# Target rows of a graph layer by one fp32 product a tile instead of three bf16 products

## The chip, the cores and the metric

The kernel runs on one core of a Trainium2 chip. The metric is the time of one execution in device microseconds.

## The reference, cut to what matters

Two graph layers stand behind each other on 3125 nodes of 256 features with 53125 edges, sorted by target node (`dst`). The change lies in the first layer, where each edge needs the projected row of its source and that of its target:

```python
ZU = jnp.einsum('nd,kdr->knr', Z, U)          # K=4 heads of R=16, so 64 numbers a node
zs = ZU[:, src, :]
zd = ZU[:, dst, :]
logits = (zs * zd).sum(-1) / scale
seg_max = jax.vmap(lambda l: jax.ops.segment_max(l, dst, num_segments=N))(logits)
exp_l = jnp.exp(logits - seg_max[:, dst])
seg_sum = jax.vmap(lambda e: jax.ops.segment_sum(e, dst, num_segments=N))(exp_l)
alpha = exp_l / (seg_sum[:, dst] + 1e-16)
agg = jax.vmap(lambda w_: jax.ops.segment_sum(w_, dst, num_segments=N))(alpha[..., None] * zs)
```

A dense gradient step and a layer norm follow on the nodes. The second layer sums rows of neighbours and runs a GRU cell on them.

## The kernel before

The nodes are cut into 25 windows (t = 0 to 24) of W = 125 targets. Since the edges are sorted by target, the edges of a window are one piece of the list, of at most SPAN = 2304, worked on as C = 18 tiles of 128 edges. The program is unrolled over the windows, `overlapped(attend)` on DVE and ACT and a plain loop on TensorE, and each engine has its order written out. Buffers alternate between two halves, h = t % 2.

In the first layer, for each window:

- GpSimd (`gather`, L638) fetches the source rows `zs` with one indirect transfer a tile, 18 a window, as soon as the indices `sidx` of the window are there. DVE writes those of window t + 2 (`sources`, L963) behind V of window t.
- SyncE (`prefetch`, L490 and L492) loads the target numbers of a window, the same row into 125 partitions (`dst_bc[h]`, 1125 KB), and pieces of them (`halo_i`). It waits for the one-hot of window t before it loads window t + 2 and then stores the finished rows of window t (`store_h2`, L509) before it turns to the next.
- DVE makes from `dst_bc[h]` the transposed one-hot `ohT` in bf16 (`target_one_hots`, L924), 125 nodes by 2304 edges. There is one such buffer. It also splits the 64-number rows of the window's own nodes, fp32, into three bf16 parts whose sum they are (`split_rows`, L929 to L937, five operations, each waiting for the one before it). Both are done one window ahead.
- TensorE multiplies the one-hot of each tile with the three parts and adds them up in fp32 (`target_rows`, L1600): 54 products for a window, into banks 0, 1 and 2. This picks each edge's target row.
- DVE `attend`: in three chunks of 8, 8 and 2 tiles it multiplies source and target rows (L954) and sums by head into `L` (L957). Between the chunks stands the end of the preceding window (`renew`, `shift`, L1057 to L1071). TensorE turns L (L1609), DVE runs two scans for the segment maxima (L995, L997, L1001), makes the next window's one-hot (L924), a remainder for the second layer (L915) and, once TensorE has turned the maxima back (L1612), the difference (L1008). ACT takes the exponential (L1334). DVE scales the source rows with it into V (L1013), writes indices (L963), compares neighbours for the next window (L941), and makes the node one-hots `oh` of the next window (L892).
- TensorE behind L1612: the dense part (L1637), the next window's target rows (L1600), and the aggregation `oh` by V (L1623, 18 products), which waits for V and for `oh` of its own window.
- DVE waits for that sum (L1038), divides, and starts the first chunk of the next window (L954).

In the last window TensorE has no target rows to make, and DVE makes two long one-hots of the second layer (L907) ahead of the first chunk. In the first window DVE splits weights for the second layer ahead of it. TensorE's queue in the first layer is thus: turn a row (L1630), L1609, L1612, L1637, L1600, L1623, L1641, L1643.

## Time and profile before

| | |
|---|---|
| time, median of 3 runs | 1218.3 us (1218.26 to 1241.45) |
| time of the profiled execution | 1217.22 us |
| its span, first to last instruction | 1215.6 us |
| busy: TensorE products, loads | 853.1 us (70%), 640.5 us (53%) |
| busy: DVE, ACT, GpSimd | 682.5 us (56%), 293.9 us (24%), 563.5 us (46%) |
| first layer's windows, about | 137 to 799 us |
| first-layer gathers on GpSimd (L638) | 450, 534.5 us busy |
| target rows (L1600) | 1350 products, 85.3 us busy |
| one-hot for them (L924) | 25, 35.3 us busy |

A product's weight load is a record of its own (PEld) and runs beside products. An fp32 product of this kernel leaves two records of each kind where a bf16 product leaves one: L1623 has 18 products a window and 36 records. In a row of the timeline, x is the number of records that were merged, and the bracket is the idle time of the engine in front of them with what ended it; "issue" is no wait that the profile shows. The two levels of TensorE's clock are 1.2 and 2.4 GHz; 0.5 and 1.0 stand for them in a stretch.

### The profile page before, as it was taken

Reading aid. Unit: us, or ns where it says so; the run is one execution under the profiler, and the core shown is the slowest. Engines: PE = TensorE matmul, PEld = TensorE weight load, DVE = VectorE, ACT = ScalarE, POOL = GpSimd, SP = SyncE. Lnnn points to the kernel's source line nnn. Section 1 sums busy time; section 2 is a strip of 40 time slices with the busy share of each in tenths; the row PEclk is TensorE's granted clock in tenths of the full one; section 3 lists DMA queues with packets and bytes.
Section 4 is the critical chain, followed back from the end, with each engine's and each line's share of the span. In section 5 each row is a group of like instructions: output and inputs, shape, how many; then the busy total and the mean of one; then the engine's idle time right before and its main releaser. Section 6 shows DMA issues by size and latency. Waiting matters only on the chain.

```text
span 1215.6 us, 14336 instructions
## 1 busy us (share of the span) xinstructions
PE 853.1 (70%) x5247; PEld 640.5 (53%) x5247; DVE 682.5 (56%) x1264; ACT 293.9 (24%) x621; POOL 563.5 (46%) x495
## 2 busy tenths in 40 slices
PE   0451656667655666665556666569999999999997
PEld 0341444456544455544445555446666666676764
DVE  4452566664565664455556555545566666555562
ACT  5230111111111111111111111224333333344331
POOL 3537277787778787777787877300000000000000
PEclk9985655555555555555555555569999999999999
DMA  4226233334333333332333331000000000000000
GB/s 126 79 48 128 81 72 69 73 79 95 73 70 71 73 81 82 78 68 68 71 71 74 80 84 35 12 13 18 17 15 16 13 18 17 18 17 18 18 14 14
DMA packets 42545, 65.97 MB, mean 54 GB/s; under 512 B 14247, under 2 KB 31696, under 8 KB 39350
## 3 DMA queue, kind: packets, MB, share of 16 engines
q1 hardware_dynamic: 24843, 48.23, 12.0%
q0 software_dynamic: 16576, 16.76, 11.0%
q8 instruction: 42, 0.69, 0.3%
q14 instruction: 28, 0.23, 0.1%
q10 hardware_dynamic: 1056, 0.07, 0.1%
HBM read 57.69 MB, written 7.20 MB: 53 GB/s over the span
## 4 chain that ended last, share of the span: by engine, by line
POOL 42%; PE 35%; issue 13%; DVE 4%; SPq 3%; DMA 2%; ACT 1%; POOLq 0%; DVEq 0%; ACTq 0%
POOL shared L638 40%; PE bank L1671 11%; PE bank L1670 5%; PE bank L1714 4%; PE bank L1721 4%; PE bank L1655 3%; PE bank L1722 2%; PE bank L1715 2%; DVE layer L1076 1%; DVE layer L1078 1%; POOL oh L712 1%; PE bank L1519 1%; PE bank L1682 1%; DMA layer<-in_edges,row_at 1%; DMA rels<-in_L_gnn_relvectors 1%
## 5 line engine op out<-in xcount | busy, mean ns | idle before, releaser
L638 POOL DMA_INDIRECT shared<-zu_table,sidx x450 | 534.5, 1188 | 162.9 <-issue 136.5
L1623 PE MATMUL bank<-layer,oh 128*125 128x84 f32 x900 | 192.1, 412 | 0.0
L1623 PEld LDWEIGHTS bank<-layer,oh 128*125 128x125 f32 x900 | 187.9, 326 | 0.0
L1600 PE MATMUL bank<-zu,shared 125*128 125x64 bf16 x1350 | 85.3, 238 | 78.8 <-issue 43.5
L1600 PEld LDWEIGHTS bank<-zu,shared 125*128 125x128 bf16 x1350 | 74.7, 127 | 102.4 <-issue 102.3
L1038 DVE TENSOR_SCALAR den<-bank 125x4 f32<-125x4 f32 x25 | 4.1, 162 | 189.9 <-issue 129.7
L1609 PE MATMUL bank<-ident,L 128*72 128x128 f32 x75 | 21.0, 417 | 125.6 <-DVE L L957 68.8
L1076 DVE COPY layer<-bank 125x256 f32<-125x256 f32 x25 | 10.6, 424 | 141.0 <-PE bank L1671 141.0
L907 DVE TENSOR_TENSOR shared<-iota_b,key_col 128x3125 bf16<-128x3125 bf16 x25 | 85.2, 3409 | 0.0
L907 DVE TENSOR_TENSOR oh<-iota_b,low_col 128x3125 bf16<-128x3125 bf16 x25 | 85.2, 3409 | 0.0
L1609 PEld LDWEIGHTS bank<-ident,L 128*72 128x72 f32 x75 | 9.4, 159 | 135.6 <-DVE L L957 73.8
L1362 ACT ACTIVATE cnt_rows<-meansT 51x125 bf16<-51x125 f32 x25 | 7.6, 305 | 281.7 <-issue 175.7
L1655 PEld LDWEIGHTS bank<-shared,oh 128*125 128x125 bf16 x625 | 61.7, 142 | 23.9 <-issue 10.0
L1655 PE MATMUL bank<-shared,oh 128*125 128x125 bf16 x625 | 66.5, 225 | 10.0 <-issue 9.0
L1671 PE MATMUL bank<-wide,zus 125*125 125x512 bf16 x208 | 73.3, 389 | 0.0
L1392 ACT ACTIVATE zus<-bank 125x500 bf16<-125x500 f32 (+1 forms) x91 | 60.3, 688 | 41.8 <-PE bank L1655 41.8
L1392 ACT ACTIVATE shared<-bank 125x500 bf16<-125x500 f32 (+1 forms) x84 | 55.8, 685 | 50.3 <-PE bank L1655 50.3
L1671 PE MATMUL bank<-wide,shared 125*125 125x512 bf16 x192 | 65.6, 379 | 0.0
L892 DVE SCALAR_TENSOR_TENSOR oh<-iota_w,win_first,dst_col 128x2250 f32<-128x2250 f32 x25 | 63.8, 2552 | 0.0
L954 DVE TENSOR_TENSOR layer<-shared,bank 128x512 f32<-128x512 f32 (+1 forms) x75 | 41.2, 549 | 37.1 <-DMA shared<-zu_table,sidx 33.3
L1670 PE MATMUL bank<-wide,zus 125*125 125x256 bf16 x195 | 54.3, 278 | 0.0
L1714 PE MATMUL bank<-whhT,layer 128*125 128x512 f32 x100 | 51.1, 593 | 0.0
(227 smaller groups left out, 1513.4 us busy)
## 6 DMA issues: line engine op xcount, KB each, us to landing
shared<-in_edges SPq DMA_DIRECT2D x25, 1125.0 KB
shared<-zu_table,sidx POOLq DMA_INDIRECT x450
xs<-in_x SPq DMA_DIRECT2D x5, 625.0 KB
h_table<-h2s SPq DMA_DIRECT2D x25, 125.0 KB
h2s<-h_table SPq DMA_DIRECT2D x25, 125.0 KB
out_dram<-layer SPq DMA_DIRECT2D x25, 125.0 KB
halo_i<-in_edges SPq DMA_DIRECT2D x25, 108.6 KB
zu_table<-zus SPq DMA_DIRECT2D x5, 156.2 KB
```

The costliest lines, as they stand in the source:

```text
L638: nc.gpsimd.indirect_dma_start(out=to(h, j), out_offset=None, in_=table, in_offset=bass.IndirectOffsetOnAxis(ap=sidx[:, h, j:j + 1], axis= ...
L892: nc.vector.scalar_tensor_tensor(o, in0, win_first[:, bass.ds(t, 1)], col, ALU.add, ALU.is_equal).then_inc(oh_made, 1)
L907: nc.vector.tensor_tensor(to.rearrange("p (g w) -> p g w", g=BW), io, col[:, t * BW:(t + 1) * BW].unsqueeze(2).broadcast_to([128, BW, W]), ...
L954: nc.vector.tensor_tensor(prod[:, a * KR:b * KR], zs[h][:, a * KR:b * KR], ps(c, 128, 0, (b - a) * KR), ALU.mult).then_inc(prod_made, 1)
L1392: nc.scalar.activation(many[t % 2].rearrange("p (a g d) -> p g a d", a=NW, g=BW)[:, a:b, :, :], ps((7, 1)[g % 2], W, 0, (b - a) * W).rearr ...
L1600: last = mm(ps(c, 128, (j - a) * KR, (j - a + 1) * KR), ohT[:, j * 128:(j + 1) * 128], zu3[:, m, :], start=m == 0, stop=m == 2)
L1623: last = mm(ps(5, W, 0, SUMS), oh[:, h, j * W:(j + 1) * W], V[:, j, :], start=j == 0, stop=j == C - 1)
L1655: last = mm(ps((7, 1)[g % 2], W, (k - a) * W, (k - a + 1) * W), lows[t % 2][:, k * W:(k + 1) * W], keys[t % 2][:, k * W:(k + 1) * W], star ...
L1670: mm(ps(0, W, 0, D), own, v[:, 2, :], start=False, stop=False)
L1671: last = mm(ps(0, W, 0, 2 * D), own, v[:, 0:2, :].rearrange("p m d -> p (m d)"), start=a == 0, stop=a == NW - 1)
L1714: mm(ps(rzb, W, 0, 2 * D), h2T[:, c * W:(c + 1) * W], whhT[:, c, 0:2 * D], start=False, stop=False)
L1721: mm(ps(rzb, W, 0, 2 * D), redT[:, c * W:(c + 1) * W], wihT[:, c, 0:2 * D], start=False, stop=c == CH - 1)
```

## The change

The one-hot is written as fp32 over the target numbers that it is made from: `ohT[h]` is `dst_bc[h]`, read as fp32. So there are two of them now. The five operations of `split_rows`, their buffers `zu3` and `rest` and their semaphore are gone. `target_rows` multiplies each tile's fp32 one-hot with the window's fp32 rows `zus`, one product a tile, 18 for a window. Since the next load into `dst_bc[h]` would now overwrite the one-hot, SyncE waits for the third chunk's target rows instead of the one-hot, and ACT's `keep_many` (second layer) waits for the same.

```diff
@@ -108,7 +108,7 @@
         dfar = part(W, at + 1024, EF, int32)
 
         dst_bc = [part(W, h * SPAN, SPAN, int32) for h in range(2)]
-        ohT = part(W, 2 * SPAN, SPAN // 2).bitcast(bf16)
+        ohT = [v.bitcast(fp32) for v in dst_bc]
         zs = [part(128, 3 * SPAN + h * C * KR, C * KR) for h in range(2)]
         assert 3 * SPAN + 2 * C * KR <= 2 * C * D
 
@@ -140,8 +140,6 @@
 
         SUMS = KR + K + RELS
         layer = sb("layer", [128, 3440])
-        zu3 = sb("zu3", [W, 3, KR], bf16)
-        rest = sb("rest", [W, 2, KR])
         prod, V, cut = carve(layer, (128, 128, K * C), (C * KR, (C, SUMS), (2, HALO)))
         cntT, h2T, redT, rz, nn, dd, outs, redS = carve(layer, (KR + RELS + 1, 128, 128, W, W, W, W, W),
                                                         ((2, W), CH * W, CH * W, (2, 2 * D), D, D, (2, D), D))
@@ -512,7 +509,7 @@
 
 
             def prefetch(t, h):
-                sp.wait_ge(oht_made, t + 1)
+                sp.wait_ge(zd_made[2], t + 1)
                 sp.wait_ge(cut_raw, t + 1)
                 load_window(t + 2, h)
                 if t == 0:
@@ -921,20 +918,7 @@
 
             def target_one_hots(t, i, h):
                 dve.wait_ge(l_bc[h], 16 * (i + 1))
-                nc.vector.tensor_scalar(ohT, dst_bc[h], node_id[0:W, bass.ds(t, 1)], None, ALU.is_equal).then_inc(oht_made, 1)
-
-            def split_rows(t):
-
-                zt = flat(zus[:, :, :], t, KR)
-                nc.vector.tensor_copy(zu3[:, 0, :], zt).then_inc(zu3_made, 1)
-                dve.wait_ge(zu3_made, 5 * t + 1)
-                nc.vector.tensor_tensor(rest[:, 0, :], zt, zu3[:, 0, :], ALU.subtract).then_inc(zu3_made, 1)
-                dve.wait_ge(zu3_made, 5 * t + 2)
-                nc.vector.tensor_copy(zu3[:, 1, :], rest[:, 0, :]).then_inc(zu3_made, 1)
-                dve.wait_ge(zu3_made, 5 * t + 3)
-                nc.vector.tensor_tensor(rest[:, 1, :], rest[:, 0, :], zu3[:, 1, :], ALU.subtract).then_inc(zu3_made, 1)
-                dve.wait_ge(zu3_made, 5 * t + 4)
-                nc.vector.tensor_copy(zu3[:, 2, :], rest[:, 1, :]).then_inc(zu3_made, 1)
+                nc.vector.tensor_scalar(ohT[h], dst_bc[h], node_id[0:W, bass.ds(t, 1)], None, ALU.is_equal).then_inc(oht_made, 1)
 
             def find_cuts(i, h):
                 dve.wait_ge(l_halo[h], 16 * (i + 1))
@@ -1007,8 +991,6 @@
                 dve.wait_ge(mT_made, t + 1)
                 nc.vector.tensor_tensor(dif[:, :], L[:, 1:C + 1, :].rearrange("p j k -> p (j k)"),
                                         ps(4, 128, 0, K * C), ALU.subtract).then_inc(dif_made, 1)
-                if not last:
-                    split_rows(t + 1)
                 dve.wait_ge(P_made, t + 1)
                 nc.vector.tensor_tensor(V[:, :, 0:KR].rearrange("p j (k r) -> p j k r", k=K),
                                         zs[h].rearrange("p (j k r) -> p j k r", k=K, r=R),
@@ -1098,7 +1080,6 @@
 
             def windowed():
                 target_one_hots(0, 0, 0)
-                split_rows(0)
                 find_cuts(0, 0)
                 one_hots(0, 0)
                 relation_one_hots(0)
@@ -1383,8 +1364,6 @@
 
                 a, b = fives(g)
                 if t == 0 and g == 0:
-                    act.wait_ge(zu3_made, 5 * NW)
-                elif t == 1 and g == 0:
                     act.wait_ge(zd_made[2], NW)
                 elif g == 0:
                     act.wait_ge(sum_made, t - 1)
@@ -1593,12 +1572,10 @@
             def target_rows(t):
 
                 pe.wait_ge(oht_made, t + 1)
-                pe.wait_ge(zu3_made, 5 * t + 5)
                 for c, (a, b) in enumerate(CHUNKS):
                     for j in range(a, b):
-                        for m in range(3):
-                            last = mm(ps(c, 128, (j - a) * KR, (j - a + 1) * KR), ohT[:, j * 128:(j + 1) * 128],
-                                      zu3[:, m, :], start=m == 0, stop=m == 2)
+                        last = mm(ps(c, 128, (j - a) * KR, (j - a + 1) * KR), ohT[t % 2][:, j * 128:(j + 1) * 128],
+                                  flat(zus[:, :, :], t, KR), start=True, stop=True)
                     last.then_inc(zd_made[c], 1)
 
             def attend(t, h, ahead):
```

TensorE, first layer, behind the turned maxima of window 0 (names as in the program; line numbers of after are 23 lower there). Before:

```order
L1612 MATMUL bank<-ident,segmax 128x72 [waits segmax_made]
L1637 MATMUL bank<-VV,hTw_own 125x256 [waits hTw_kept]
L1637 MATMUL bank<-VV,hTw_own 125x256
L1600 MATMUL bank<-zu,shared 128x64 [waits zu3_made,oht_made]
L1600 MATMUL bank<-zu,shared 128x64 x53
L1623 MATMUL bank<-layer,oh 125x84 [waits V_made,ohk_made,oh_made]
L1623 MATMUL bank<-layer,oh 125x84 x17
```

After:

```order
L1589 MATMUL bank<-ident,segmax 128x72 [waits segmax_made]
L1614 MATMUL bank<-VV,hTw_own 125x256 [waits hTw_kept]
L1614 MATMUL bank<-VV,hTw_own 125x256
L1577 MATMUL bank<-zus,shared 128x64 [waits oht_made]
L1577 MATMUL bank<-zus,shared 128x64 x17
L1600 MATMUL bank<-layer,oh 125x84 [waits V_made,ohk_made,oh_made]
L1600 MATMUL bank<-layer,oh 125x84 x17
```

The 54 products are 18 now, and the first of them waits for the one-hot alone. Nothing else in the queue moves.

DVE, window 1, from the difference to the wait for the aggregated sum. Before:

```order
L1008 TENSOR_TENSOR dif<-L,bank 128x72 [waits mT_made]
L929 CAST zu<-zus 125x64
L931 TENSOR_TENSOR rest<-zus,zu 125x64 [waits zu3_made]
L933 CAST zu<-rest 125x64 [waits zu3_made]
L935 TENSOR_TENSOR rest<-rest,zu 125x64 [waits zu3_made]
L937 CAST zu<-rest 125x64 [waits zu3_made]
L1013 TENSOR_TENSOR layer<-shared,layer 128x18x64 [waits P_made]
L963 COPY sidx<-src_col 128x18 [waits V_made]
L941 TENSOR_TENSOR layer<-halo_i 72x385 [waits l_halo0]
L892 SCALAR_TENSOR_TENSOR oh<-iota_w,win_first,dst_col 128x2250
```

After:

```order
L992 TENSOR_TENSOR dif<-L,bank 128x72 [waits mT_made]
L995 TENSOR_TENSOR layer<-shared,layer 128x18x64 [waits P_made]
L947 COPY sidx<-src_col 128x18 [waits V_made]
L925 TENSOR_TENSOR layer<-halo_i 72x385 [waits l_halo0]
L889 SCALAR_TENSOR_TENSOR oh<-iota_w,win_first,dst_col 128x2250
```

The five operations are gone from between the difference and V; the order of the rest is the same.

SyncE, between the store of one window's rows and the load of a window two further on. Before:

```order
L509 DMA h_table<-h2s 125x256 [waits h2_made]
L488 TENSOR_LOAD starts [waits st_h2,cut_raw,oht_made]
L488 ISA x2
L490 ISA
L490 DMA shared<-in_edges 125x2304
```

After:

```order
L506 DMA h_table<-h2s 125x256 [waits h2_made]
L485 TENSOR_LOAD starts [waits st_h2,cut_raw,zd_made2]
L485 ISA x2
L487 ISA
L487 DMA shared<-in_edges 125x2304
```

Only the semaphore waited for is another one.

## Rows read from the trace of the kernel before

**Rows 1.** The page, 40 equal slices: TensorE's granted clock in tenths.
```profile
PEclk9985655555555555555555555569999999999999
```

**Rows 2.** The page, chain that ended last: share of the span by engine and line.
```profile
POOL shared L638 40%; PE bank L1671 11%; PE bank L1670 5%; PE bank L1714 4%; PE bank L1721 4%; PE bank L1655 3%; PE bank L1722 2%; PE bank L1715 2%; DVE layer L1076 1%; DVE layer L1078 1%; POOL oh L712 1%; PE bank L1519 1%; PE bank L1682 1%; DMA layer<-in_edges,row_at 1%; DMA rels<-in_L_gnn_relvectors 1%
```

**Rows 3.** Timeline, one early window: start us, us, engine, line, operation.
```profile
287.50 0.28 DVE L954 TENSOR_TENSOR layer<-shared,bank 128x128 f32<-128x128 f32 x1
...
290.55 1.41 DVE L924 TENSOR_SCALAR shared<-shared,node_id 125x2304 bf16<-125x2304 int32 x1
...
290.86 2.00 PE L1637 MATMUL bank<-VV,hTw_own 128*125 128x256 f32 x4
...
292.47 0.26 ACT L1334 ACTIVATE layer<-dif 128x72 f32<-128x72 f32 x1 [3.45 <-issue]
...
293.61 1.34 DVE L1013 TENSOR_TENSOR layer<-shared,layer 128x1152 f32<-128x1152 f32 x1
...
293.84 1.86 PE L1600 MATMUL bank<-zu,shared 125*128 125x64 bf16 x32 [0.98 <-DVE zu L937]
...
294.00 0.01 SPq L490 DMA_DIRECT2D shared<-in_edges  x1
...
295.62 2.55 DVE L892 SCALAR_TENSOR_TENSOR oh<-iota_w,win_first,dst_col 128x2250 f32<-128x2250 f32 x1
...
298.69 7.84 PE L1623 MATMUL bank<-layer,oh 128*125 128x84 f32 x36
...
306.56 0.16 DVE L1038 TENSOR_SCALAR den<-bank 125x4 f32<-125x4 f32 x1 [8.06 <-issue]
...
308.16 0.68 DVE L954 TENSOR_TENSOR layer<-shared,bank 128x512 f32<-128x512 f32 x1
...
312.56 0.28 DVE L954 TENSOR_TENSOR layer<-shared,bank 128x128 f32<-128x128 f32 x1
```

**Rows 4.** Timeline, two later windows, DVE: the start of the third chunk.
```profile
390.82 0.29 DVE L954 TENSOR_TENSOR layer<-shared,bank 128x128 f32<-128x128 f32 x1 [1.04 <-DMA shared<-zu_table,sidx]
...
417.80 0.29 DVE L954 TENSOR_TENSOR layer<-shared,bank 128x128 f32<-128x128 f32 x1 [1.18 <-DMA shared<-zu_table,sidx]
```

**Rows 5.** Timeline, DVE: third chunks of windows 1, 23, 24; end of the last.
```profile
162.92 0.28 DVE L954 TENSOR_TENSOR layer<-shared,bank 128x128 f32<-128x128 f32 x1
...
741.51 0.29 DVE L954 TENSOR_TENSOR layer<-shared,bank 128x128 f32<-128x128 f32 x1 [1.18 <-DMA shared<-zu_table,sidx]
...
759.40 0.16 DVE L1038 TENSOR_SCALAR den<-bank 125x4 f32<-125x4 f32 x1 [7.33 <-PE bank L1623]
...
767.65 0.68 DVE L954 TENSOR_TENSOR layer<-shared,bank 128x512 f32<-128x512 f32 x1
...
773.57 0.29 DVE L954 TENSOR_TENSOR layer<-shared,bank 128x128 f32<-128x128 f32 x1 [1.52 <-DMA shared<-zu_table,sidx]
```

**Rows 6.** Groups of instructions: busy us, mean ns of one, idle before.
```profile
L1623 PE MATMUL bank<-layer,oh 128*125 128x84 f32 x900 | 192.1, 412 | 0.0
...
L1637 PE MATMUL bank<-VV,hTw_own 128*125 128x256 f32 x100 | 50.0, 653 | 0.0
...
L1519 PEld LDWEIGHTS bank<-setup 128*125 128x125 f32 x100 | 12.8, 188 | 3.9 <-DVE setup L825 3.5
```

**Rows 7.** Timeline, loads of the stationary side in the projections of setup.
```profile
53.43 0.51 PEld L1519 LDWEIGHTS bank<-setup 128*125 128x125 f32 x4
```

**Rows 8.** Timeline, the first window's dense part and aggregation.
```profile
143.94 1.92 PE L1637 MATMUL bank<-VV,hTw_own 128*125 128x256 f32 x4
...
148.43 4.01 PEld L1623 LDWEIGHTS bank<-layer,oh 128*125 128x125 f32 x36
...
152.63 0.16 DVE L1038 TENSOR_SCALAR den<-bank 125x4 f32<-125x4 f32 x1 [1.84 <-PE bank L1623]
```

**Rows 9.** Busy us by engine in a stretch of the first window, then TensorE's clock.
```profile
147.00:149.00 2.00, 2.00 (x52) 2.00 (x50) 1.90 (x4) 0.53 (x1) 0.37 (x1) 0.89 0.04 8
```

**Rows 10.** GpSimd's gathers by tile: ns of one, least, median and most.
```profile
L638 POOL DMA_INDIRECT shared<-zu_table,sidx x450: 940/944/3277, 78.6 to 770.1; - x150
```

More of the change, by code:

```diff
@@ L346, in gnn_kernel @@
         oh_made = sem("oh_made")
-        zu3_made = sem("zu3_made")
+        any_in = sem("any_in")
         ohk_made = sem("ohk_made")
@@ L386, in gnn_kernel @@
         out_made = sem("out_made")
-        any_in = zu3_made
         any_cast = cut_raw
```

## The prediction

> **What bounds the kernel now.** I read the page first. Its chain of what ended last gives GpSimd's gathers (L638) 40% of the span, then TensorE's second-layer products [rows 2]. The change touches only the first layer, so the question is what sets the pace of its 25 windows. Each window has a DVE piece `attend`, which needs the 18 gathered tiles of its window in three chunks (L954), and a TensorE piece. I call the start of the third, small chunk (L954, 128x128) c2 and measure one window from c2 to the next.
>
> The timeline of one early window [rows 3], c2 at 287.50, next c2 at 312.56, shows a closed circle with no gather in it: segment maxima, L924 (290.55 to 291.96), TensorE's dense part L1637 from 290.86, target rows L1600 from 293.84, aggregation L1623 from 298.69, DVE's L1038 at 306.56, first chunk 308.16, c2 312.56. No row there waits for a transfer. This circle takes 25.06 us. Ten windows on, c2 has 1.18 us of idle time in front of it that a gather's landing ended [rows 4]: there GpSimd sets the pace, and c2 comes after 26.98 us (390.82 to 417.80). So the two bounds lie 2 us apart: GpSimd starts with a lead, the circle eats it for about eight windows, then the gathers bind. From the first to the last but one window c2 goes from 162.92 to 741.51: 22 windows in 578.6 us, 26.3 each; the last takes 32.06, since two long one-hots of the second layer stand in it [rows 5].
>
> **The change, part by part.** (1) DVE loses five small operations per window between L1008 (dif) and L1013. L1013 starts at 293.61; the exponential that it also needs ends at 292.73 [rows 3], so it can start about 0.6 to 0.9 us sooner. That alone moves neither bound: L1013 and L892 (ends 298.17) leave DVE idle until 306.56. It is not on the circle unless TensorE becomes free first.
>
> (2) L924 now writes fp32 over its own int32 input. It takes 1.41 us for 2304 elements, 1.6 elements a nanosecond; L892, with two inputs in fp32, takes 2.55 us for 2250 [rows 3]. I take 1.41 (one input, 4-byte input as before); the other bound is 2.6. With 1.41 the one-hot is there at 291.96, before TensorE is free.
>
> (3) SyncE's prefetch waits for the target rows of its own window, where it waited for the one-hot. Both are made one window before SyncE gets there, since it stands behind the store of the preceding window's rows: nothing. At the start it waits for target rows 0, which end while the weights are still loading: nothing.
>
> (4) TensorE: 54 bf16 products become 18 fp32 ones. An fp32 product is two records here: L1623 has 18 a window and 36 records, 7.84 us at the low clock level. Taking off the last one (0.41, the group's mean), one record costs 7.43/35 = 0.212 us [rows 3, 6]. Those have 84 columns, the new ones 64. Does the width matter? At the high level, the loads of records of 64 columns (L1519) follow each other by (0.51 - 0.19)/3 = 0.107 us, those of L1623's 84 columns by (4.01 - 0.19)/35 = 0.109 [rows 7, 8]; 0.19 is a single load at that level [rows 6]. So the stationary side sets the rate, not the columns. That side is 128 wide instead of 125: 0.212 x 128/125 = 0.217, and 36 of them 7.8 us. The lower bound is the rate by columns, 64/84 of it, 0.162 or 5.8 us; below that is 3.9 us, where 64 columns cost half of what 128 would.
>
> The Trainium skill ("TensorE: Matmul & The Clock Gate", Weight-path perf modes) says that the fast weight load needs 128 weights and a type that is not fp32, so this change gives it up; its section LDWEIGHTS gives about P/1.2 ns, 107 ns for 128. By 107 ns a record the 36 would take 3.9 us; by the row they take 7.8.
>
> Now the circle. TensorE is free after L1637: start 290.86, four records at (2.00 - 0.65)/3 = 0.45 [rows 3, 6], so 292.66, which is c2 + 5.16. Before, L1600 stood there until 298.69 (c2 + 11.19), in part because it waited until 293.84 for the parts, and because only 32 of its products came at once and 22 late. After: target rows c2 + 5.16 to 12.97; aggregation as before 306.56 - 298.69 = 7.87, to 20.84; L1038 to the first chunk 1.60; first chunk to c2 4.40. Sum 26.84 us, against 25.06. One-hots L892 are made long before (c2 + 10.7), so the circle runs through TensorE alone there.
>
> Windows 1 to 23: 22 x 26.84 = 590.5, against 578.6: **+11.9**. Last window: 12.97 + 7.87 + (767.65 - 759.40 = 8.25) + 4.40 = 33.49, against 32.06: **+1.4**. First window: L1637 starts 143.94, free at 145.74; the clock is at its low level until about 147.2 to 147.4 and then at the high one (0.89 on average over 147 to 149) [rows 8, 9]. Some 8 records at 0.217 and 28 at 0.109 x 128/125 = 0.112 end at 150.6, where the aggregation had begun at 148.43: **+2.2** (if the clock stays low, 153.5 and an aggregation of 7.87 instead of 152.63 - 148.43 = 4.20: +8.7). Sum +15.5 on the profiled 1217.2, that is 1232.7; the median of the runs is 1.1 above the profiled run: 1233.8, rounded to **1233**. Since 26.84 is about GpSimd's own 27.0, which also gets a little shorter, gathers no longer bind: they wait for indices.
>
> **Rivals.** *A, slower: TensorE is starved of instructions.* L1600 runs 32 products at 58 ns; the other 22, some 1.3 us at that rate, fill the 3 us until 298.69. The hole of 1.7 us lies right behind the issue of the 1125 KB destination row at 294.00 [rows 3]. If the fp32 train meets the same hole it loses up to 1.7 us a window: 23 x 1.7 = +39, so 1273. It counts as slower by 2% from (1242.7 - 1233.8)/23 = 0.39 us a window. Against it: 32 products had run before the hole, and 32 fp32 records take 7 us, longer than the hole lasts. A one-hot of 2.6 us instead of 1.41 belongs here too: it ends at 293.15, +0.5 a window, 1245.
>
> *B, not slower: the clock rises.* The page has the clock at 5 tenths through the whole first layer, though L1623 runs 7.8 us without a break [rows 1, 3]; only in the first window does it rise, right behind L1637 and L1600 [rows 9]. The new train has no gap behind L1637. If it were at the high level, target rows take 4.0 and the aggregation 4.2, the circle is about 20, and GpSimd binds everywhere. GpSimd works without a pause either way, so c2 of the last window stays at 773.57 less what the shorter DVE block gives back: a gather takes 0.94 us in the median and up to 3.28 [rows 10], the long ones beside DVE's block from L924 to L892, and that block is 0.6 us shorter in 22 windows: 0 to 14 us. Time 1203 to 1218, say 1211. The Trainium skill (same page, The HAM clock gate) says that sustained activity releases the throttle. By that rule the longer train would warm it; here L1623's 7.8 us do not, so I give it little.
>
> *C, not slower: a record is cheap at 64 columns* (3.9 us for the train). Then TensorE is done at c2 + 9.1, DVE's one-hots at about c2 + 10.1 gate the aggregation, the circle is 24, GpSimd binds as in B: 1211. At 5.8 us the circle is 24.8, the same. The two rates in [rows 7, 8] speak against it.
>
> **How the numbers follow.** My forecast (circle of about 26.8, 1222 to 1246 with the first window and 0.01 us of error a record): 0.63. A 0.16, B 0.13, C 0.08. The range takes in B's and C's middle and A's near end: 1209 to 1248. A change of 2%, 24 us, is about what a measurement of this kernel tells from none: slower is A, less the part below its threshold, and the tail of mine, 0.19; faster needs B or C with more relief than 14 us, 0.03; the same, 0.78.
>
> **What would show it.** In the changed profile: fp32 target rows in 36 records, 7.8 us, starting 0.1 to 0.3 us behind L1637; c2 to c2 near 26.8 in all windows from the second on, none at 25; no wait of L954 for a gather; GpSimd waiting for `sidx` in most windows; L1038 about 2 us later behind c2. Wrong would be: records under 0.19 us (C), a clock of 1.0 in the first layer (B), gaps inside the train (A). The second layer should take the same time.

## The result, and the profile after

The changed kernel takes 1365.8 us (median of 6 runs, 1360.8 to 1377.0) where the kernel before takes 1220.2 us (6 runs, 1217.3 to 1241.5): a ratio of 1.121 with the 95% interval [1.116, 1.126]. The ratio leaves out the run of before at 1241.5 us, one of the chip's slower executions. It is 12% slower. 1233 us and the range 1209 to 1248 us were wrong. The side of rival A came true, but the time lies 132 us above the forecast, more than three times A's price of 39 us.

The profiled run of after takes 1365.1 us, its span 1363.4 us against 1215.6 us. Its page still shows the low clock level through the whole first layer, as [rows 1] does:

```profile
PEclk9965655555555555555555555555999999999999
```

The groups of instructions of after (busy us, mean ns of one, then the idle time of the engine just before them and what ended it):

```profile
L635 POOL DMA_INDIRECT shared<-zu_table,sidx x450 | 486.1, 1080 | 328.3 <-DVE sidx L947 194.0 <-issue 129.8 <-DMA zu_table<-zus 4.5
...
L1577 PE MATMUL bank<-zus,shared 125*128 125x64 f32 x900 | 194.1, 417 | 27.6 <-issue 27.5
...
L979 DVE TENSOR_TENSOR_SCAN runs<-cutf,bank 72x256 f32<-72x256 f32 x25 | 17.1, 683 | 137.0 <-remote 128.6 <-issue 5.7 <-PE bank L1586 2.8
```

The first says that GpSimd now waits for indices, 194.0 us in total, as forecast. The second is the new fp32 train: 900 records, 36 a window. The third is what no step of the prediction had: the scan L979 (L995 before), which reads the transposed logits, has 137.0 us of idle time in front of it, 5.5 us a window, and most of it is put down to "remote", a semaphore whose sender the profile does not name at that time. The same group before has 25.1 us:

```profile
L995 DVE TENSOR_TENSOR_SCAN runs<-cutf,bank 72x256 f32<-72x256 f32 x25 | 17.1, 683 | 25.1 <-issue 20.9 <-PE bank L1609 4.3
```

One window of after, from third chunk to third chunk, answers to [rows 3]:

```profile
303.45 0.28 DVE L938 TENSOR_TENSOR layer<-shared,bank 128x128 f32<-128x128 f32 x1
...
304.10 0.86 PE L1586 MATMUL bank<-ident,L 128*72 128x128 f32 x3 [3.09 <-DVE L L941]
...
307.52 0.94 POOL L635 DMA_INDIRECT shared<-zu_table,sidx  x1 [0.30 <-issue]
308.75 0.68 DVE L979 TENSOR_TENSOR_SCAN runs<-cutf,bank 72x256 f32<-72x256 f32 x1 [4.70 <-issue]
...
310.25 1.41 DVE L921 TENSOR_SCALAR shared<-shared,node_id 125x2304 f32<-125x2304 int32 x1
...
310.56 2.00 PE L1614 MATMUL bank<-VV,hTw_own 128*125 128x256 f32 x4
...
312.36 7.78 PE L1577 MATMUL bank<-zus,shared 125*128 125x64 f32 x36
...
312.46 1.36 DVE L995 TENSOR_TENSOR layer<-shared,layer 128x1152 f32<-128x1152 f32 x1 [0.33 <-ACT layer L1315]
...
314.87 3.32 POOL L635 DMA_INDIRECT shared<-zu_table,sidx  x1 [6.41 <-DVE sidx L947]
...
319.93 7.80 PE L1600 MATMUL bank<-layer,oh 128*125 128x84 f32 x36
...
328.37 0.16 DVE L1020 TENSOR_SCALAR den<-bank 125x4 f32<-125x4 f32 x1 [11.00 <-PE bank L1600]
...
334.37 0.28 DVE L938 TENSOR_TENSOR layer<-shared,bank 128x128 f32<-128x128 f32 x1
...
338.45 0.94 POOL L635 DMA_INDIRECT shared<-zu_table,sidx  x1 [0.30 <-issue]
341.73 0.68 DVE L979 TENSOR_TENSOR_SCAN runs<-cutf,bank 72x256 f32<-72x256 f32 x1 [6.77 <-remote]
```

The transposes L1586 are recorded from 304.10, but the scan that waits for their semaphore starts at 308.75, 4.70 us behind VectorE's last operation. In the next window it is 6.77 us. In the kernel before this wait is 0.95 us in every window from the second on. The reader should also see the gathers: those for one window run from 314.87 to 339.39 (the last row of GpSimd, 338.45 + 0.94) as one burst of 18, and the scan starts 2.34 us behind its end. In the window before it starts 0.29 us behind the end of the last gather (307.52 + 0.94 = 308.46). In windows 2 to 23 the scan waits between 4.70 and 7.50 us.

Where the 147.8 us of span went is read from the third chunks of windows 0, 1, 23 and 24. Those of before are in [rows 5], with 139.22 for window 0:

```profile
146.23 0.28 DVE L938 TENSOR_TENSOR layer<-shared,bank 128x128 f32<-128x128 f32 x1
...
177.10 0.28 DVE L938 TENSOR_TENSOR layer<-shared,bank 128x128 f32<-128x128 f32 x1
...
883.93 0.28 DVE L938 TENSOR_TENSOR layer<-shared,bank 128x128 f32<-128x128 f32 x1
...
921.54 0.28 DVE L938 TENSOR_TENSOR layer<-shared,bank 128x128 f32<-128x128 f32 x1
```

| stretch | before, us | after, us | difference | forecast |
|---|---|---|---|---|
| start to window 0 | 139.22 | 146.23 | +7.0 | 0 |
| window 0 to 1 | 23.70 | 30.87 | +7.2 | +2.2 |
| window 1 to 23 (22 windows) | 578.59 | 706.83 | +128.2 | +11.9 |
| window 23 to 24 | 32.06 | 37.61 | +5.6 | +1.4 |
| window 24 to the end | 442.0 | 441.9 | -0.2 | 0 |

A window takes 706.83 / 22 = 32.13 us, where 26.84 was forecast. The 7.0 us ahead of window 0 need not be the change's: three further kernels with the same fp32 train (e2, e4 and e5 below) reach window 0 at 137.2 to 139.4 us, as before, and e9, which has the bf16 train of before, reaches it at 146.8 us. Why that start differs between kernels stays open.

### The profile page after: what moved, and what is told of

It is laid out like the page before. It is cut to its first block, busy times and chain, and to the rows that moved or that the text cites. A ratio compares the mean times of both kernels' runs of the same rounds, so it can differ in the third digit from the quotient of the medians.

```text
span 1363.4 us, 13287 instructions
## 1 busy us (share of the span) xinstructions
PE 960.6 (70%) x4797; PEld 766.9 (56%) x4797; DVE 656.9 (48%) x1139; ACT 293.8 (22%) x621; POOL 515.2 (38%) x495
## 3 DMA queue, kind: packets, MB, share of 16 engines
q0 software_dynamic: 16576, 16.76, 7.0%
## 4 chain that ended last, share of the span: by engine, by line
PE 61%; DVE 15%; another core or an unknown queue 9%; issue 8%; SPq 2%; DMA 2%; POOL 1%; ACT 1%; DVEq 0%; ACTq 0%
PE bank L1600 14%; PE bank L1577 13%; PE bank L1648 10%; PE bank L1647 5%; PE bank L1614 3%; PE bank L1691 3%; PE bank L1698 3%; DVE layer L938 3%; PE bank L1632 3%; PE bank L1699 2%; PE bank L1692 2%; DVE L L941 1%; DVE runs L979 1%; DVE runs L981 1%
## 5 line engine op out<-in xcount | busy, mean ns | idle before, releaser
L635 POOL DMA_INDIRECT shared<-zu_table,sidx x450 | 486.1, 1080 | 328.3 <-DVE sidx L947 194.0
L1577 PEld LDWEIGHTS bank<-zus,shared 125*128 125x128 f32 x900 | 197.0, 332 | 32.6 <-issue 27.6
L1577 PE MATMUL bank<-zus,shared 125*128 125x64 f32 x900 | 194.1, 417 | 27.6 <-issue 27.5
L1600 PE MATMUL bank<-layer,oh 128*125 128x84 f32 x900 | 195.0, 417 | 0.0
L1600 PEld LDWEIGHTS bank<-layer,oh 128*125 128x125 f32 x900 | 192.0, 332 | 0.0
L1020 DVE TENSOR_SCALAR den<-bank 125x4 f32<-125x4 f32 x25 | 4.0, 162 | 274.5 <-PE bank L1600 254.5
L1589 PE MATMUL bank<-ident,segmax 72*128 72x72 f32 x25 | 9.5, 378 | 154.3 <-DVE segmax L985 148.1
L1589 PEld LDWEIGHTS bank<-ident,segmax 72*128 72x128 f32 x25 | 4.5, 181 | 165.3 <-DVE segmax L985 158.6
L979 DVE TENSOR_TENSOR_SCAN runs<-cutf,bank 72x256 f32<-72x256 f32 x25 | 17.1, 683 | 137.0 <-remote 128.6
L1586 PE MATMUL bank<-ident,L 128*72 128x128 f32 x75 | 21.0, 418 | 86.2 <-DVE L L941 72.5
L1586 PEld LDWEIGHTS bank<-ident,L 128*72 128x72 f32 x75 | 9.4, 159 | 96.3 <-DVE L L941 80.7
## 6 DMA issues: line engine op xcount, KB each, us to landing
h_table<-h2s SPq DMA_DIRECT2D x25, 125.0 KB
h2s<-h_table SPq DMA_DIRECT2D x25, 125.0 KB
out_dram<-layer SPq DMA_DIRECT2D x25, 125.0 KB
```

Source lines behind the costliest of these rows:

```text
L635: nc.gpsimd.indirect_dma_start(out=to(h, j), out_offset=None, in_=table, in_offset=bass.IndirectOffsetOnAxis(ap=sidx[:, h, j:j + 1], axis= ...
L1577: last = mm(ps(c, 128, (j - a) * KR, (j - a + 1) * KR), ohT[t % 2][:, j * 128:(j + 1) * 128], flat(zus[:, :, :], t, KR), start=True, stop= ...
L1600: last = mm(ps(5, W, 0, SUMS), oh[:, h, j * W:(j + 1) * W], V[:, j, :], start=j == 0, stop=j == C - 1)
```

## The experiments

All times below are one run each, unless said otherwise; the kernel before took 1211.6 to 1227.9 us beside them, but 1252.2 us beside e1 to e4. A window is again the mean from window 1 to window 23, and "scan wait" is the idle time in front of the first scan.

| kernel | us | a window, us | scan wait, sum of 25, us |
|---|---|---|---|
| after | 1365.1 | 32.1 | 137.0 |
| e1 72 small products behind the train | 1668.7 | 45.6 | 25.1 |
| e2 16 small products behind the transposes | 1279.9 | 28.8 | 26.5 |
| e3 before, one bf16 product of three | 1222.4 | 26.3 | 24.5 |
| e4 own one-hot, old wait of SyncE | 1377.9 | 32.9 | 148.4 |
| e5 no gathers | 1231.0 | 26.6 | 24.9 |
| e6 half the gathers | 1242.7 | 27.0 | 24.9 |
| e7 16 small products ahead of the transposes | 1395.5 | 33.7 | 177.7 |
| e8 before, fp32 train, split kept | 1404.2 | 34.0 | 140.3 |
| e9 before, six fp32 products more | 1347.2 | 31.8 | 62.0 |
| e10 a pause in each burst | 1279.2 | 28.6 | 54.6 |
| e11 1 small product behind | 1363.8 | 32.8 | 146.9 |
| e12 4 small products behind | 1378.3 | 32.7 | 144.1 |
| e13 plain DMAs for gathers | 1231.6 | 26.6 | 24.4 |
| e14 16 behind both transposes | 1393.4 | 33.5 | 125.0 |
| e15 36 plain half DMAs | 1232.3 | 26.6 | 25.2 |

**Is it the edit's small parts? e4 and e8.** The edit of e4:

```
-        ohT = [v.bitcast(fp32) for v in dst_bc]
+        ohT = [part(W, 2 * SPAN, SPAN)] * 2
...
-                sp.wait_ge(zd_made[2], t + 1)
+                sp.wait_ge(oht_made, t + 1)
```

> The changed kernel with the fp32 one-hot in a buffer of its own (the words behind the two index rows) and SyncE's prefetch waiting for the one-hot as before, instead of for the target rows; the output is the same. Theory W (SyncE's new wait or the writing in place sets off the stall): the scan waits 0.95 us, c2 to c2 about 26.8, total about 1235 to 1245. Theories S, F and Q: as the changed kernel, the scan waits 5 to 7 us, total within 10 us of 1365.

Measured 1377.9 us, scan wait 148.4 us. Neither the writing in place nor SyncE's new wait does it.

e8 is the kernel before with TensorE's part of the change alone:

```
-        ohT = part(W, 2 * SPAN, SPAN // 2).bitcast(bf16)
+        ohT = part(W, 2 * SPAN, SPAN)
...
-                        for m in range(3):
-                            last = mm(..., ohT[:, j * 128:(j + 1) * 128], zu3[:, m, :], start=m == 0, stop=m == 2)
+                        last = mm(..., ohT[:, j * 128:(j + 1) * 128], flat(zus[:, :, :], t, KR), start=True, stop=True)
```

> The kernel before with the fp32 target rows alone: one fp32 one-hot in a buffer of its own and one fp32 product per tile, while the five split operations stay (their output unused) and TensorE still waits for them, and SyncE waits as before. So TensorE's part of the change without VectorE's and SyncE's. Theories G and F: the stall behind L1609 (the transposes) appears here too, since the circle through TensorE is longer than the gathers' 27.0 us: the scan waits 5 to 7 us, c2 to c2 about 28.0 + 5 = 33 us (the train starts 1.2 us later, behind the parts), total 1365 to 1400. If removing the split moved something that matters: scan wait 0.95, c2 to c2 28.0, total about 1265.

Measured 1404.2 us, 34.0 us a window, scan wait 140.3 us. The longer train on TensorE, with its one-hot in fp32, is enough. e4 has the same one-hot buffer and the same wait of SyncE, but no split: 32.9 us a window. So taking the split away gave some 1.1 us a window back, by one run of each.

**Is it fp32, or the number of instructions? e1, e3, e9.** e1 adds behind the target rows

```
+                for _ in range(72):
+                    mm(ps(7, 8, 0, 4), iota_b[:, 0:8], iota_b[:, 0:4], start=True, stop=True)
```

> The changed kernel with 72 tiny bf16 products (8 x 4 outputs, into a bank that the first layer leaves alone) behind the 18 target-row products of each window; nothing else changes and the output is the same. It restores about the number of TensorE instructions that a window had before (54 loads and 54 products there, 36 records now). At the 58 ns a record of the bf16 train of before they cost some 4.2 us a window. Theory S (TensorE's instruction supply: the stall behind the scan's transposes L1586, 4.7 to 7.5 us in the changed kernel, depends on how many instructions a window has): the wait of the scan L979 goes back to 0.95 us, c2 to c2 is about 26.8 + 4.2 = 31.0 us, total about 1345. Theory F (the fp32 train itself leaves TensorE slow) and theory W (SyncE's new wait, or the one-hot written over the indices): the scan still waits 5 to 7 us, c2 to c2 is about 36, total about 1365 + 25 x 4.2 = 1470.

Both theories missed: the scan no longer waits (25.1 us in 25 windows), but the kernel takes 1668.7 us. Its timeline, TensorE's products in one window (an L1581 row is the added products, L1602 the aggregation) and the window's last gather:

```profile
434.68 1.39 PE L1581 MATMUL bank<-iota_b 128*8 128x4 bf16 x50
436.52 0.26 PE L1581 MATMUL bank<-iota_b 128*8 128x4 bf16 x5 [0.45 <-issue]
437.26 0.26 PE L1581 MATMUL bank<-iota_b 128*8 128x4 bf16 x5 [0.47 <-issue]
438.72 0.24 PE L1581 MATMUL bank<-iota_b 128*8 128x4 bf16 x4 [1.20 <-issue]
...
453.07 0.94 POOL L635 DMA_INDIRECT shared<-zu_table,sidx  x1 [0.30 <-issue]
...
457.20 3.87 PE L1602 MATMUL bank<-layer,oh 128*125 128x84 f32 x18 [0.23 <-issue]
```

Fifty products run in 1.39 us; then they come in small groups whose starts lie 0.7 or 1.4 us apart, though they wait for no semaphore. The aggregation behind them goes on in the same way, one to four records at a time, until 457.20, where 18 records follow each other without a gap. TensorE is held up for some 20 us, for want of instructions as it looks, and this lies on the gathers: they run from 429.48 to 454.01, and TensorE is back at its pace 3.2 us behind their end. The hold-up is of the kind that rival A named. The scan is spared because it now lies elsewhere.

e3 takes instructions away from the kernel before:

```
-                        for m in range(3):
+                        for m in range(1):
```

> The kernel before, with its five split operations and its bf16 one-hot, but only the first of the three bf16 products per tile (18 instead of 54): the two lower parts of the rows are left out of the sum. Few TensorE instructions, no fp32 train, SyncE's wait as before. Theory S: the scan waits 5 to 7 us here too, c2 to c2 about 24.6 + 5.2 = 29.8 us, total about 1280 to 1290. Theories F and W: the scan waits 0.95 us, the gathers set the pace (27.0 us a window), total 1210 to 1220.

Measured 1222.4 us, scan wait 24.5 us, windows of 26.9 us that end on a gather. Theory S (few instructions make the stall) falls. A window is 26.3 us, as before; the total stands beside a run of before of 1252.2 us and is not compared with it. e9 lengthens the kernel before, bf16 train and all:

```
                     last.then_inc(zd_made[c], 1)
+                for _ in range(6):
+                    mm(ps(7, 128, 0, D), ident[:, :], VV[:, 0, :], start=True, stop=True)
```

> The kernel before, its three bf16 products and its split untouched, with six fp32 products of 256 columns (24 instructions, at 0.43 us a record 5.2 us) behind the target rows, into a bank that is free. It makes the circle through TensorE longer than the gathers' 27.0 us without any fp32 target rows: 25.06 + 5.2 = 30.2 us. Theory G (the stall comes when a burst of 18 gathers, started behind the index copy at about c2 + 10, ends just about where the transposes of the next window stand): it appears here too, the scan waits 4 to 7 us, c2 to c2 is 34 to 36 us, total about 1400. Theory F (fp32 target rows are needed for it): the scan waits 0.95 us, c2 to c2 28.5 to 30.2 us, total about 1290.

Measured 1347.2 us. Theory G gave 1400, F 1290. The stall is there with a bf16 train, in 12 of 25 windows in front of the scan. One of them, and the end of the window behind it:

```profile
203.95 0.86 PE L1611 MATMUL bank<-ident,L 128*72 128x128 f32 x3 [3.09 <-issue]
...
207.32 0.94 POOL L638 DMA_INDIRECT shared<-zu_table,sidx  x1 [0.30 <-issue]
...
211.39 0.68 DVE L995 TENSOR_TENSOR_SCAN runs<-cutf,bank 72x256 f32<-72x256 f32 x1 [7.49 <-remote]
...
247.80 4.06 PE L1625 MATMUL bank<-layer,oh 128*125 128x84 f32 x36
...
265.52 0.16 DVE L1038 TENSOR_SCALAR den<-bank 125x4 f32<-125x4 f32 x1 [22.44 <-remote]
```

The second place is larger than the scan's. VectorE's L1038 reads the aggregated sum, whose records end at 247.80 + 4.06 = 251.86, and starts at 265.52, 13.7 us later; in other windows this is up to 18 us. (The ends of TensorE's records are modelled by the profile, their starts are not; all 36 had started by 251.9.) So fp32 target rows are not needed, and where the stall falls depends on the program around it. ScalarE is hit as well:

```profile
466.55 0.38 ACT L1357 ACTIVATE hTw_own<-bank 128x250 f32<-128x250 f32 x1 [2.74 <-issue]
```

It reads rows whose transposing TensorE's record ends at 457.48. In e2 VectorE's L995, which waits for ScalarE, starts 0.03 us behind it in the middle of a burst of gathers. So what comes late is what TensorE sends, and not VectorE's own start.

The total of 1400 was too high, at least in part because the circle under the stalls is not the 30.2 us that was expected. TensorE's clock is at its high level for a part of the first layer:

```profile
PEclk9965766666666665667575666667999999999999
```

The aggregation takes 4.06 us here against 7.80 in after, and several windows with little or no wait take 21.9 to 23.8 us. So the stall came though the undisturbed circle is shorter than the gathers' 27.0 us.

**Is it the gathers? e5, e6, e10.** e5 leaves out the gathers from window 2 on, e6 every second one; in e5:

```
                     for j in range(a, b):
+                        if i and True:
+                            continue
```

(`i and j % 2` in e6, with the thresholds of VectorE's waits to match.)

> The changed kernel without the gathers of windows 2 to 24 (only windows 0 and 1 are gathered; the later ones use their rows again, so that part of the computation is left out). Theory G (while GpSimd issues its gathers back to back, TensorE is hardly supplied with new instructions; in the changed kernel the wait of the scan ends 0.3 to 3.0 us behind the last gather of a burst of 18, e.g. 308.46 and 308.75, or 696.24 and 697.24): no stall, the scan waits 0.95 us in every window, c2 to c2 26.8 us, total about 1235. Theory F (the long fp32 train sets it off by itself): the stall stays at 5 to 7 us, total about 1365.

> The changed kernel with every second gather left out from window 2 on (9 instead of 18 a window; the other tiles keep old rows, so that part of the computation is left out). Theory G: the burst is about 13 us long and over before the next transposes L1586, so the scan waits 0.95 us and c2 to c2 is 26.8 us, total about 1235 to 1245. Theory F: stall of 5 to 7 us as in the changed kernel, total about 1365.

Measured 1231.0 and 1242.7 us. The group of the first scan in e5:

```profile
L981 DVE TENSOR_TENSOR_SCAN runs<-cutf,bank 72x256 f32<-72x256 f32 x25 | 17.1, 684 | 24.9 <-PE bank L1588 24.9
```

and one window of its timeline, from third chunk to third chunk:

```profile
249.02 0.28 DVE L940 TENSOR_TENSOR layer<-shared,bank 128x128 f32<-128x128 f32 x1
...
252.39 2.00 PE L1616 MATMUL bank<-VV,hTw_own 128*125 128x256 f32 x4
...
261.75 7.80 PE L1602 MATMUL bank<-layer,oh 128*125 128x84 f32 x36
...
269.59 0.16 DVE L1022 TENSOR_SCALAR den<-bank 125x4 f32<-125x4 f32 x1 [10.40 <-PE bank L1602]
...
275.59 0.28 DVE L940 TENSOR_TENSOR layer<-shared,bank 128x128 f32<-128x128 f32 x1
```

The circle is 26.57 us in nearly all windows. The stall is gone without a change on TensorE, VectorE or SyncE, and what is left is the circle that the prediction summed (26.84). Theory F falls; G stands, and its number was hit within 4 us. With half the gathers the scan's wait is gone as well. What stays in 17 windows of e6 is 0.5 to 0.7 us between the aggregation's end and VectorE's L1022, where e5 has 0.04 (27.0 against 26.6 us a window).

e10 leaves all gathers in, and parts each burst:

```
                 for c, (a, b) in enumerate(CHUNKS):
+                    if c == 1 and n > 1:
+                        pool.wait_ge(meansT_made, n - 1)
```

> The changed kernel with one wait more on GpSimd: behind the first 8 gathers for window t + 2 it waits for the turned sums of window t (meansT), at about c2 + 22.5, so the burst of 18 falls into 8 and 10 with a pause of 1 to 3 us, and its end moves from c2 + 35 to about c2 + 36. The output is the same. Theory G with a supply that recovers in a pause: the scan waits 0.95 us again, c2 to c2 27 to 28.5 us, total 1240 to 1280. Theory G in which only the end of all gathers brings relief: the stall stays or grows by 1 to 2 us, total 1365 to 1400.

Measured 1279.2 us, 28.6 us a window. Two windows of its timeline, the scans and the gathers beside them:

```profile
279.52 0.94 POOL L637 DMA_INDIRECT shared<-zu_table,sidx  x1 [0.91 <-issue]
...
287.51 0.68 DVE L981 TENSOR_TENSOR_SCAN runs<-cutf,bank 72x256 f32<-72x256 f32 x1 [3.35 <-remote]
...
309.18 0.94 POOL L637 DMA_INDIRECT shared<-zu_table,sidx  x1 [3.50 <-DVE meansT L1036]
...
314.78 0.68 DVE L981 TENSOR_TENSOR_SCAN runs<-cutf,bank 72x256 f32<-72x256 f32 x1 [0.95 <-PE bank L1588]
```

Ahead of the first scan GpSimd paused only 0.91 us, and the scan waits 3.35 us. Ahead of the second it paused 3.50 us, and the scan waits 0.95 us. Most windows of this kernel alternate so. From window 1 to 23, a pause of 1.7 to 3.6 us goes with a scan wait of 0.95 us every time, one of 0.9 to 1.0 us with 2.6 to 4.5 us, and the one window without a pause has 9.04 us. So a pause of some 2 us lets TensorE recover; and the first of the two scans starts while gathers still run, so the end of a burst is not the only thing that brings relief.

**What does the semaphore wait for? e2, e7, e11, e12, e14.** All add the small products of e1 to the changed kernel, 16 behind the transposes (e2), 16 ahead of them (e7), 1 and 4 behind (e11, e12), 16 behind and 16 more behind L1589 (e14). In e2:

```
                 last.then_inc(LT_made, 1)
+                for _ in range(16):
+                    mm(ps(7, 8, 0, 4), iota_b[:, 0:8], iota_b[:, 0:4], start=True, stop=True)
```

> The changed kernel with 16 tiny bf16 products right behind the three transposes L1586, ahead of TensorE's wait for the segment maxima; the output is the same. Theory Q (the transposes are done at once, but their semaphore is posted only when TensorE gets at its next instructions): with instructions that wait for nothing right behind, the semaphore comes at once, the scan L979 waits 0.95 us again, c2 to c2 about 27, total about 1245. Theories S, F and W: the stall stays at 5 to 7 us and the total within 10 us of 1365; in S the place of the stall can shift by some instructions.

> The changed kernel with 16 tiny bf16 products ahead of TensorE's wait for the last logits, that is ahead of the transposes L1586, where e2_pad_behind_LT had them behind; TensorE is idle for 3.5 us there. The output is the same. Theory Q (the transposes' semaphore is posted only when the next instructions have come; the pads behind supplied them): the stall stays, 5 us or more, total 1365 or longer. If only the count or the alignment of the instructions matters: the stall goes as in e2, total about 1280.

> The changed kernel with a single tiny bf16 product (one load, one product) behind the transposes L1586, where e2 had 16. If the next instruction is all that the transposes' semaphore waits for, 1 works like 16: the scan waits 0.95 us, total about 1280. If the pads help by their number (16 pads are 32 instructions of supply), one does next to nothing: the scan waits 5 to 7 us, total 1360 to 1370.

> As e11, with four pads. If the next instruction is all that is waited for: as e2, about 1280. If the number counts in proportion: an eighth to a quarter of e2's gain or so, total 1340 to 1365.

> The changed kernel with 16 tiny bf16 products behind the transposes L1586, as in e2, and 16 more behind the transpose of the segment maxima L1589. In e2 the first semaphore came on time and the second, which VectorE's L992 waits for, came 4 to 11 us late. If about 32 instructions behind a semaphore bring it on time: both are on time, c2 to c2 about 27.5 us, total 1245 to 1260. If the pads only move a shortage of instructions on: L992 or another wait is late still, holes in the train grow, total 1280 or more.

e2 gave 1279.9 us and seemed to bear out theory Q, that the semaphore comes with the next instructions. e7 gave 1395.5, which fits as well. But e2's groups of the first scan and of L992, which waits for the next transpose, show that e2 only moved the stall:

```profile
L979 DVE TENSOR_TENSOR_SCAN runs<-cutf,bank 72x256 f32<-72x256 f32 x25 | 17.1, 683 | 26.5 <-issue 17.1 <-PE bank L1586 6.7 <-remote 2.7
...
L992 DVE TENSOR_TENSOR dif<-L,bank 128x72 f32<-128x72 f32 x25 | 5.7, 229 | 139.8 <-remote 139.8
```

L992 has no wait in after (0.0 us); here it has 139.8 us, some of it hidden, since the train runs beside it. One window of the same timeline:

```profile
228.65 0.38 PE L1591 MATMUL bank<-ident,segmax 72*128 72x72 f32 x1 [1.21 <-issue]
...
230.62 5.64 PE L1577 MATMUL bank<-zus,shared 125*128 125x64 f32 x26
...
234.79 0.23 DVE L992 TENSOR_TENSOR dif<-L,bank 128x72 f32<-128x72 f32 x1 [4.54 <-remote]
```

The transpose is recorded at 228.65, its reader starts at 234.79, and meanwhile the train is recorded from 230.62: later instructions do not bring a semaphore at once. With 1 and 4 products the times are 1363.8 and 1378.3 and the scan waits as in after, and with 16 at both places 1393.4. Theory Q falls. Products of this kind shift which semaphore is late; they cure nothing.

**Is it any DMA from GpSimd? e13, e15.** From window 2 on each indexed gather becomes a plain DMA of the same tile:

```
+                            nc.gpsimd.dma_start(to(h, j), table[j * 128:(j + 1) * 128, :]).then_inc(done[h][c], 16)
```

> The changed kernel in which, from window 2 on, each of the 18 indexed gathers is a plain DMA of GpSimd of the same size (128 consecutive rows of 256 bytes into the same tile, so the wrong rows are fetched and that part of the computation is changed), in the same places and behind the same wait. If any burst of DMAs that GpSimd issues holds TensorE up: the scan waits 4 to 7 us as in the changed kernel, total about 1365 (less if the burst is shorter). If it is what GpSimd does for an indexed gather (0.94 us each): the scan waits 0.95 us, c2 to c2 26.6 us, total about 1231 as without gathers.

> As e13, but each tile is fetched by two plain DMAs of 64 rows instead of one of 128, so 36 issues a window (again the wrong rows from window 2 on: that part of the computation is changed). At e13's 0.53 us an issue the run lasts some 19 us, from c2 + 10 to c2 + 29, past the transposes of the next window at c2 + 26.6. If a long unbroken run of DMA issues on GpSimd's queue is enough: the scan waits for 2 us or more and c2 to c2 is 28 us or more, total 1265 or more. If it takes the indexed form: 0.95 us, c2 to c2 26.6 us, total about 1232.

Measured 1231.6 and 1232.3 us, scan wait 24.4 and 25.2 us, as without gathers, though the page of e13 has the same 16576 packets on that queue as after. GpSimd's rows in e13's groups, and one window of e15's timeline with 36 issues:

```profile
L641 POOL DMA_DIRECT2D shared<-zu_table x414 | 218.7, 539 | 399.3 <-DVE sidx L950 391.6 <-issue 7.7
```

```profile
310.81 10.32 POOL L642 DMA_DIRECT2D shared<-zu_table  x20 [8.13 <-DVE sidx L952]
321.72 8.19 POOL L642 DMA_DIRECT2D shared<-zu_table  x16 [0.58 <-issue]
```

A plain issue takes 0.54 us, an indexed one 1.08 in the mean. The 36 issues of e15 (29824 packets on that queue) fill 310.81 to 329.91 with one gap of 0.6 us, to about 1.0 us ahead of the next transposes, and no semaphore is late. They lie over the whole aggregation, and L1025, which reads its sum, starts 0.04 us behind it as in e5, where after has 0.6 to 0.75 us in nearly all windows. In e9's window above the late semaphore came 3.1 us behind the end of its gathers, so a hold-up by e15's run should have reached the scan; but no plain issue was still running at the transposes, and that case stays untested. As far as these runs go, the hold-up belongs to the indexed gathers, not to the packets or to a long run of issues as such.

## Why the prediction was wrong

**The bound and the forecast of gathers** held: L954's wait for a gather is gone, GpSimd waits for indices in 23 windows (194.0 us), and the circle runs through TensorE.

**(1) The split** went as forecast: L995 starts at 312.46, 0.03 us behind the end of the exponential, where the kernel before had 0.88. e8 against e4 prices it: with the split kept a window costs 1.1 us more.

**(2) The one-hot** takes 1.41 us in fp32 and in place, as taken.

**(3) SyncE's wait** costs nothing (e4).

**(4) The fp32 train** is 36 records, and the aggregation behind it starts 319.93 - 312.36 = 7.57 us later: 0.210 us a record against 0.217. The load does not pay for 128 instead of 125. The Trainium skill ("TensorE: Matmul & The Clock Gate", LDWEIGHTS) gives P/1.2 ns for P columns; an estimate from that is 3.9 us for the train, and at the low clock level this trace has twice that. The circle so summed was 26.84 us, and 26.57 us is measured where nothing disturbs it (e5). Rivals B and C did not come: the clock stays at its low level, and no record is cheap. (The sum of 1233.8 us should have been rounded to 1234; it changes nothing.)

**First window**: +7.2 instead of +2.2. The fallback in step 4 was +8.7 with the clock low, and that is nearly what came: the train takes 7.35 us there, the aggregation 7.80.

```profile
151.64 7.35 PE L1577 MATMUL bank<-zus,shared 125*128 125x64 f32 x36
...
158.78 7.80 PE L1600 MATMUL bank<-layer,oh 128*125 128x84 f32 x36
```

TensorE's clock by stretch, the third number from the end of a row (1 is 2.4 GHz, 0.50 is 1.2 GHz), shows the fall to the low level:

```profile
146.00:156.00 10.00, 7.25 (x38) 0.82 0.01 1
156.00:176.00 20.00, 12.96 (x55) 0.50 0.14 26
```

The level in this window differs between kernels of the same train: in e11 it is the high one from 137 to 155 us, and window 0 to 1 takes 24.1 us, below the forecast 25.9. No run says why, so the first window's term was a guess at the level, by one trace.

**The step that failed** is the part of the circle taken over unchanged: c2 to the dense part, 287.50 to 290.86 = 3.36 us in [rows 3]. After has 303.45 to 310.56 = 7.11 us in a good window; e5, without gathers, has 252.39 - 249.02 = 3.37. The term holds the scan's wait of 0.95 us, which the prediction does not name and which went into the sum as a constant. It became 4.7 to 7.5 us: 137.0 - 25.1 = 112 us, of 147.8. A smaller one of the same kind stands behind the aggregation: from its start to VectorE's L1020 it is 328.37 - 319.93 = 8.44 us, where e5, without gathers, has 269.59 - 261.75 = 7.84 and before 7.87 [rows 3]; 0.6 us in 22 windows are 13 us. The circle itself adds 6 (22 x 26.57 = 584.5 against 578.6) and 1 in the last window, the first window 7.2, the start 7.0: 146 of 147.8 us.

**The cause**, as far as the runs show it: GpSimd's indexed gathers hold TensorE up, in what the profile shows as late semaphores (after, e2) or as starts 0.7 us apart (e1). Taking the gathers away or making them plain ends it (e5, e13, e15), halving them ends all but 0.6 us of it (e6), and pauses in them ease it (e10). The gathers alone are not enough: before and e3 run under them and their scans wait 0.95 us. The sentence "gathers no longer bind: they wait for indices" saw the trigger and took it for a relief. In the kernel before GpSimd works almost without a pause, but beside VectorE's block from L924 to L892 two or three gathers of each window are 1.7 to 3.3 us long, and no more than some 14 short ones stand in a row. After, the gathers wait for `sidx` at the end of that block, so they come as one burst of 18, of which only the first is long (3.32 us at 314.87); 17 short ones follow. It covers the aggregation and ends 5.0 us behind the next c2 (339.39 - 334.37), on top of the transposes, a place of the circle where nothing runs beside the wait. That the row of short gathers without a break is what counts is argued from these rows and from e10; no other run varied it. Two other ways of giving TensorE more work do the same: e8 by fp32, e9 by six unrelated products.

**Rival A** named the starving of TensorE and had 0.16. Its place, inside the train, and its price, at most the hole's 1.7 us a window, were read off the kernel before, where the train has slack behind it. That hole looks like e1's: its products, too, start 0.7 us apart, beside a gather of 3.24 us.

```profile
296.87 0.21 PE L1600 MATMUL bank<-zu,shared 125*128 125x64 bf16 x1 [1.17 <-issue]
297.59 1.29 PE L1600 MATMUL bank<-zu,shared 125*128 125x64 bf16 x21 [0.51 <-issue]
```

The prediction put it down to the destination row issued at 294.00. No run shows that, and e5 issues the same row beside its fp32 train and has no such hole. "Longer than the hole lasts" was the wrong test: e1's hole is 20 us long.

**Still open** is what the two engines share. The Trainium skill ("Runtime: NRT & Kernel Launch", Instruction fetch mechanics) holds that an engine fetches its instructions ahead through a DMA queue of its own, and that this is mostly hidden; e1's starts 0.7 us apart without any wait are not hidden, but no run shows whether they are a fetch or something behind it. Nor do the runs say how many instructions TensorE has in hand when a burst begins, or why e3 and before, under gathers with hardly a pause, lose nothing or 1.7 us.

No kernel of this study beats the one before. The undisturbed fp32 circle is 1231 us, and e3, with a third of the products, shows why less work on TensorE brings nothing either: the gathers then set 26.9 us a window.

## What to carry to other kernels

When a change takes an engine from working without a pause to working in bursts, look at what each burst now lies on, and ask whether anything there was only hidden before: the added time need not come from the work that was added. A short constant wait in the profile (0.95 us, 24 times) is a price only as long as its surroundings are the same. Where such a wait grows and neither of the two engines is busy in it, thin out or swap the suspected neighbour's work before changing the waiting engine's: e5, e6 and e13 settled in three runs what six ways of adding products could only shift.

## What the runs showed of the hardware

Not expected: a TensorE product recorded as done can have its semaphore seen 3.8 to 6.5 us late (after), and up to 18 us late (e9), while GpSimd issues indexed gathers (0.94 us each, one every 1.25 us). The wait can end up to 3.8 us behind the last of them. Plain DMAs from GpSimd did not do it (e13 with the same packets, e15). Bf16 products of 4 columns that wait for nothing then start 0.7 or 1.4 us apart in groups of 1 to 5, where fifty of them take 1.39 us undisturbed (e1). A pause of 1.7 us or more in a burst brought the wait back to 0.95 us in every window that had one (e10).
